# The expert stage of a routed layer: output norms in other places, one of them on another engine, the up-bias as one product

## The reference

```python
eid = argmax(x @ centroids.T)
alpha = sigmoid(sum(x * centroids[eid]))
xn = (x - mu) * rsqrt(var + EPS)
xln = xn * ln_g[eid] + ln_b[eid]
ffn = relu(xln @ w1[eid] + b1[eid]) @ w2[eid] + b2[eid]     # 128 -> 512 -> 128
out = x + alpha * ffn
```

## Time and profile before

| | |
|---|---|
| time, median of 3 runs | 2848.79 us (2848.25 to 2849.33) |
| the profiled execution: time, span | 2853.14 us, 2851.4 us |
| busy: PE, DVE, ACT, POOL | 2018, 1835, 1576, 1163 us |
| mean granted TensorE clock | 0.867 |
| four slots of a pass in the trace: the first scatter | 1159.4 us |
| the last scatter of the stage | 1457.8 us |

### The profile page before, as it was taken

How to read it: one execution, slowest core, us unless ns; L and a number is a source line. 1 busy time by engine, 2 the same in 40 slices (tenths; PEclk the granted TensorE clock), 3 DMA queues, 4 the chain that set the end, 5 groups by cost and what they waited for, 6 DMA issues and landing times. The chain is left out here.

```text
span 2851.4 us, 39979 instructions
## 1 busy us (share of the span) xinstructions
PE 2018.1 (71%) x11854; PEld 1037.9 (36%) x11909; DVE 1834.8 (64%) x3731; ACT 1576.2 (55%) x2903; POOL 1162.6 (41%) x718
## 2 busy tenths in 40 slices
PE   2677777777777763666646787777777777658886
PEld 0344444444444443556522222222222222124432
DVE  5565665555565522222225999999999999946665
ACT  1566666566666642444436666666666666435443
POOL 1111211211221112344325888888888878710000
PEclk7799998889899886888878899989999998878887
DMA  3000000000000001111111111112121111011111
GB/s 121 23 16 20 23 21 27 27 20 20 21 22 20 24 16 33 37 45 41 37 49 47 48 49 41 41 44 56 47 55 40 40 41 49 22 34 30 45 37 45
DMA packets 137060, 105.16 MB, mean 37 GB/s; under 512 B 12872, under 2 KB 130776, under 8 KB 136544
## 3 DMA queue, kind: packets, MB, share of 16 engines
q1 hardware_dynamic: 131424, 89.48, 11.3%
q0 software_dynamic: 5504, 13.90, 1.4%
HBM read 42.18 MB, written 27.59 MB: 24 GB/s over the span
## 5 line engine op out<-in xcount | busy, mean ns | idle before, releaser
L1738 POOL TENSOR_TENSOR hc<-h,c_rep 128x1024 f32<-128x1024 f32 x256 | 602.4, 2369 | 157.4 <-DVE h L1696 150.0
L1696 DVE TENSOR_TENSOR_SCAN h<-decay,bank 128x1024 f32<-128x1024 f32 x256 | 572.6, 2268 | 0.0
L1582 ACT ACTIVATE decay<-bank,neg_a_r 128x510 f32<-128x510 f32 x512 | 322.4, 682 | 323.4 <-PE bank L1473 275.8
L1687 DVE TENSOR_TENSOR bank<-bank,b_rep 128x1024 f32<-128x1024 f32 x256 | 304.3, 1216 | 53.7 <-PE bank L1460 53.0
L1460 PE MATMUL bank<-u,sel_u 128*128 128x512 bf16 x489 | 166.1, 421 | 234.9 <-DVE h L1696 227.9
L613 ACT ACTIVATE es<-bank 128x384 f32<-128x384 f32 x512 | 208.5, 493 | 52.9 <-PE bank L447 52.6
L1460 PEld LDWEIGHTS bank<-u,sel_u 128*128 128x128 bf16 x512 | 33.6, 99 | 408.5 <-DVE h L1696 363.7
L1473 PE MATMUL bank<-d,sel_u 128*128 128x512 bf16 x481 | 168.8, 424 | 6.4 <-ACT decay L1582 2.2
L901 POOL TENSOR_TENSOR xl<-x_in,f_mean_var 128x512 f32<-128x512 f32 x16 | 17.0, 1062 | 363.3 <-ACT f_rstd L604 363.3
L914 POOL TENSOR_TENSOR mag<-mag,one_up 128x512 f32<-128x512 f32 x16 | 20.5, 1282 | 338.7 <-ACT one_up L675 338.7
L1487 PE MATMUL bank<-hc,y_sel 128*32 128x512 f32 x1024 | 146.7, 647 | 4.6 <-POOL hc L1738 4.6
(11 more groups left out here) (333 smaller groups left out, 4727.4 us busy)
## 6 DMA issues: line engine op xcount, KB each, us to landing
xvs<-xv SPq DMA_DIRECT2D x16, 512.0 KB, 3.0
xs<-rows_in_dram SPq DMA_DIRECT2D x72, 68.0 KB
w<-in_w_dram SPq DMA_DIRECT2D x2, 2048.0 KB
x_in<-in_x_dram SPq DMA_DIRECT2D x16, 256.0 KB
xlb_dram<-xl SPq DMA_DIRECT2D x16, 256.0 KB, 2.3
xlb_m<-xlb_dram SPq DMA_DIRECT2D x16, 256.0 KB, 3.8
x_m<-in_x_dram SPq DMA_DIRECT2D x16, 256.0 KB, 3.7
g_xn<-yx_dram SPq DMA_DIRECT2D x16, 256.0 KB
```

The lines of the kernel that those rows point to most:

```text
L1582: act.activation(decay[n % 4][:, i, :, 1:], seq(DL[i])[:, :, 1:], ACT.Exp, scale=c["neg_a_r"][:, hf, g:g + 1]).then_inc(s["n_da"], 1)
L1687: dve.tensor_tensor(pair_of(BD[n % 2]), pair_of(BD[n % 2]), b_rep[p if n < NS else q][:, :].unsqueeze(1).to_broadcast([P, 2, STEP]), ALU.m ...
L1696: dve.tensor_tensor_scan(flat(h[n % 4]), decay[n % 4].rearrange("p i b t -> p (i b t)"), BD[n % 2], 0.0, ALU.mult, ALU.add).then_inc(s["n_ ...
L1738: pool.tensor_tensor(hc[n % 4][:, :, :], h[n % 4][:, :, :], c_rep[p][:, :].unsqueeze(1).to_broadcast([P, 2, STEP]), ALU.mult).then_inc(s[" ...
```

## The change

Five things, none of which alters what is computed:

1. The first norms of a pass are done two in slot 2 and two in slot 3; the sum, the row numbers and `y2` follow in slot 3 and, behind them, the four scatters.
2. The second norm is done by DVE, as (y - mean) x rstd, two in slot 1 and two in slot 2, one pass later than before: a pass has now `norm` (of pass k - 1), `again` (statistics of the sums of pass k - 2, in slot 3, with a semaphore of their own, `mv2`) and `finish` (second norm and scatter of pass k - 3). There is one pass more behind the last.
3. ACT's Ln and Exp stand ahead of slot 1's relu instead of behind its `xls`.
4. The up-bias is one product with 512 columns. `sel` is a one-row-in-32 selector, `b1_split` has the bias with one row for each expert and chunk of 128, and `b2_split` uses every fourth of these rows.
5. In `setup` b_1 is stored to DRAM and loaded back as 32 rows of 128; b_2 is loaded row by row.

```diff
-        b_2 = tmp("b_2", [E, D])
+        b_2 = tmp("b_2", [E * FC, D])
+        b_r = tmp("b_r", [E * FC, P])
         conv_rows = tmp("conv_rows", [P, TAPS, DI])
-        hi = tmp("su_hi", [E, F], bf16)
-        mid = tmp("su_mid", [E, F], bf16)
-        rest = tmp("su_rest", [E, F])
...
-            sp.dma_start(b_2[:, :], dram["b_2"]).then_inc(s["su_expert"], 16)
...
+            sp.wait_ge(s["su_blank"], 1)
+            for e in range(E):
+                sp.dma_start(b_2[FC * e:FC * e + 1, :], dram["b_2"][e:e + 1, :]).then_inc(s["su_b2"], 16)
+            sp.wait_ge(s["su_b1"], 1)
+            sp.dma_start(d["b1"], b_1[:, :]).then_inc(s["su_b1_out"], 16)
+            sp.wait_ge(s["su_b1_out"], 16)
+            sp.dma_start(b_r[:, :], d["b1"].rearrange("e (f p) -> (e f) p", p=P)).then_inc(s["su_b1_in"], 16)
...
+            dve.memset(b_2[:, :], 0.0).then_inc(s["su_blank"], 1)
...
-            chain(dve.tensor_copy(c["sel"][:, :, :], c["sel_cols"][:, 0:E].unsqueeze(2).to_broadcast([P, E, P])))
+            chain(dve.tensor_copy(c["sel"][:, :, :], c["sel_cols"].unsqueeze(2).to_broadcast([P, E * FC, P])))
...
-            chain(dve.tensor_tensor(b_1[:, :], banks[0][0:E, :], b_1[:, :], ALU.add))
-            split3(dve, chain, b_1[:, :], c["b1_split"], hi[:, :], rest[:, :], mid[:, :], E)
-            split3(dve, chain, b_2[:, :], c["b2_split"], hi[:, 0:D], rest[:, 0:D], mid[:, 0:D], E)
+            dve.tensor_tensor(b_1[:, :], banks[0][0:E, :], b_1[:, :], ALU.add).then_inc(s["su_b1"], 1)
 
             for e in range(E):
                 chain(dve.tensor_scalar(c["w_1"][:, e * F:(e + 1) * F], c["w_1"][:, e * F:(e + 1) * F],
                                         e_vec[:, e:e + 1], None, ALU.mult))
-
-
+            dve.wait_ge(s["su_b2"], 16 * E)
+            split3(dve, chain, b_2[:, :], c["b2_split"], hi[:, :], rest[:, :], mid[:, :], E * FC)
+            dve.wait_ge(s["su_b1_in"], 16)
+            split3(dve, chain, b_r[:, :], c["b1_split"], hi[:, :], rest[:, :], mid[:, :], E * FC)
...
-            chain(dve.tensor_copy(c["tile_col"][:, 1, :], of[:, :]))
+            chain(dve.tensor_scalar(c["tile_col"][:, 1, :], of[:, :], float(FC), None, ALU.mult))
...
-            one_pass(eng, 0, 0, 0, True, False, False)
-            one_pass(eng, 1, 0, 1, True, True, False)
-            one_pass(eng, 2, 0, 2, True, True, True)
+            one_pass(eng, 0, 0, 0, True, False, False, False)
+            one_pass(eng, 1, 0, 1, True, True, False, False)
+            one_pass(eng, 2, 0, 2, True, True, True, False)
             with eng.Fori(0, PASSES // 3 - 2) as n:
                 for i in range(3):
-                    one_pass(eng, n * 3 + (3 + i), n + 1, i, True, True, True)
+                    one_pass(eng, n * 3 + (3 + i), n + 1, i, True, True, True, True)
             for i in range(3):
-                one_pass(eng, PASSES - 3 + i, PASSES // 3 - 1, i, True, True, True)
-            one_pass(eng, PASSES, PASSES // 3, 0, False, True, True)
-            one_pass(eng, PASSES + 1, PASSES // 3, 1, False, False, True)
+                one_pass(eng, PASSES - 3 + i, PASSES // 3 - 1, i, True, True, True, True)
+            one_pass(eng, PASSES, PASSES // 3, 0, False, True, True, True)
+            one_pass(eng, PASSES + 1, PASSES // 3, 1, False, False, True, True)
+            one_pass(eng, PASSES + 2, PASSES // 3, 2, False, False, False, True)
...
-                ex = pe.value_load(c["tile_col"][0:1, 1, bass.ds(t, 1)], min_val=0, max_val=E - 1)
-                return col, c["sel"][:, bass.ds(ex, 1), :].rearrange("k a p -> k (a p)")
+                ex = pe.value_load(c["tile_col"][0:1, 1, bass.ds(t, 1)], min_val=0, max_val=(E - 1) * FC)
+                return col, c["sel"][:, bass.ds(ex, FC), :].rearrange("k a p -> k (a p)"), c["sel"][:, bass.ds(ex, 1), :].rearrange("k a p -> k (a p)")
...
-            def up(n, j, first, col, row):
...
                 pe.sem_inc(s["passed"], 1)
-                for f in range(FC):
-                    pe.matmul(bank[:, f * P:(f + 1) * P], c["b1_split"][:, f * P:(f + 1) * P], row, start=f == 0, stop=False, skip_group_check=True)
+                pe.matmul(bank[:, :], c["b1_split"][:, :], rows, start=True, stop=False, skip_group_check=True)
...
-            def one_pass(pool, k, third, r, main, norm, finish):
-                a, b = (r + 2) % 3, (r + 1) % 3
+            def one_pass(pool, k, third, r, main, norm, again, finish):
+                a = (r + 2) % 3
                 for j in range(SLOTS):
                     if main and not is_last(k):
                         copy(k + 1, j, False)
-                    if j == 2 and norm:
+                    if j == 3 and norm:
 
                         pool.wait_ge(s["on"], k)
                         if not (isinstance(k, int) and k < 4):
@@ -1196,11 +1205,11 @@
                         pool.tensor_copy(idx[a][:, :], xs[a][:, :, TOKEN]).then_inc(s["y2"], 1)
                     if j == 3 and finish:
 
-                        pool.wait_ge(s["xno"], k - 1)
+                        pool.wait_ge(s["xno"], k - 2)
                         pool.sem_inc(s["w_passed"], 1)
                         for i in range(SLOTS):
-                            pool.indirect_dma_start(out=d["yx"], out_offset=bass.IndirectOffsetOnAxis(ap=idx[b][:, i:i + 1], axis=0),
-                                                    in_=yx[b][:, i, :], in_offset=None).then_inc(sent[b], 16)
+                            pool.indirect_dma_start(out=d["yx"], out_offset=bass.IndirectOffsetOnAxis(ap=idx[r][:, i:i + 1], axis=0),
+                                                    in_=yx[r][:, i, :], in_offset=None).then_inc(sent[r], 16)
...
-            def one_pass(act, k, third, r, main, norm, finish):
-                a, b = (r + 2) % 3, (r + 1) % 3
+            def one_pass(act, k, third, r, main, norm, again, finish):
...
+                    if j == 1 and (norm or finish):
+
+                        if norm:
+                            act.wait_ge(s["mv"], k)
+                        if finish:
+                            act.wait_ge(s["mv2"], k - 2)
+                        act.activation(ln[:, :], mv[:, :, 1], ACT.Ln, bias=EPS).then_inc(s["ln"], 1)
+                        act.wait_ge(s["ln"], k)
+                        act.activation(rs[:, :], ln[:, :], ACT.Exp, scale=-0.5).then_inc(s["rs"], 1)
+                    if main:
...
-                    if j == 1 and (norm or finish):
-
-                        act.wait_ge(s["mv"], k)
-                        act.activation(ln[:, :], mv[:, :, 1], ACT.Ln, bias=EPS).then_inc(s["ln"], 1)
-                        act.wait_ge(s["ln"], k)
-                        act.activation(rs[:, :], ln[:, :], ACT.Exp, scale=-0.5).then_inc(s["rs"], 1)
-                    if j == 2 and norm:
-                        act.wait_ge(s["nm"], k)
-                        if not (isinstance(k, int) and k == 1):
-                            act.wait_ge(s["y2"], k - 1)
-                        for i in range(SLOTS):
+                    if j >= 2 and norm:
+                        if j == 2:
+                            act.wait_ge(s["nm"], k)
+                            if not (isinstance(k, int) and k == 1):
+                                act.wait_ge(s["y2"], k - 1)
+                        for i in (2 * j - 4, 2 * j - 3):
                             last = act.activation(on[:, i, :], o[a][:, i, :], ACT.Identity, scale=rs[:, i:i + 1], bias=nm[:, i:i + 1])
-                        last.then_inc(s["on"], 1)
-                    if j == 2 and finish:
-                        act.wait_ge(s["nm"], k)
-                        for i in range(SLOTS):
-                            last = act.activation(yx[b][:, i, D:2 * D], yx[b][:, i, 0:D], ACT.Identity,
-                                                  scale=rs[:, SLOTS + i:SLOTS + i + 1], bias=nm[:, SLOTS + i:SLOTS + i + 1])
-                        last.then_inc(s["xno"], 1)
+                        if j == 3:
+                            last.then_inc(s["on"], 1)
...
-            def one_pass(dve, k, third, r, main, norm, finish):
+            def one_pass(dve, k, third, r, main, norm, again, finish):
                 a, b = (r + 2) % 3, (r + 1) % 3
+
+                def second(i):
+                    return dve.tensor_scalar(yx[r][:, i, D:2 * D], yx[r][:, i, 0:D], mv[:, SLOTS + i, 0:1], rs[:, SLOTS + i:SLOTS + i + 1],
+                                             ALU.subtract, ALU.mult)
+
                 for j in range(SLOTS):
                     if main and not (is_last(k) and j + 2 >= SLOTS):
                         features(k, j + 2, is_first(k))
-                    if j == 0:
-                        if norm:
-                            result(k - 1, SLOTS - 1, a).then_inc(s["o_st"], 1)
-                        if finish:
-                            dve.wait_ge(s["y2"], k - 1)
-                            for i in range(SLOTS):
```

(43 more changed lines are left out.)

20 lines of the change are left out of this document (13 added, 7 removed).

## The result

| | before | after |
|---|---|---|
| median of 5 runs, us | 2849.33 (2848.25 to 2857.78) | 2837.27 (2834.74 to 2840.51) |
| ratio | 1 | 0.9953 [0.9936, 0.9970] |
| profiled execution: time, span | 2853.1, 2851.4 | 2840.15, 2838.3 |
| last row scatter of attention ends | 1079.41 | 1085.92 |
| experts' stage, first load of `xs` to first load of `g_xn` | 366.4 | 346.6 |

12.1 us saved, 0.47%, where 31.5 were forecast (2817.3): faster as said and inside the range (2798 to 2842), but less than half of what was forecast. A later set of runs of the same kernel gave 0.9940 [0.9928, 0.9951], 17 us.

The account below looks back on a forecast made before the run. The prediction took a ring between PE and ACT, lengthened by ACT's norms, to bound the experts' stage. 14 x (19.15 - 16.8) = 32.9, + 5.1 - 6.2 - 0.3 = 31.5 us saved: 2817.3 us, range 2798 to 2842.

Parts of the forecast that it names:

- What bounds the kernel: Experts' stage: no engine's busy time but a ring between PE and ACT, lengthened by ACT's output norms; 19.15 us a pass.
- (1): ACT without second norms (1.54 us a pass): tile 2 to tile 3 becomes 3.97 us, the boundary to tile 0 stays 4.73.
- (2): Ln and Exp ahead of tile 1's relu: Exp done at 7.3 us, relu possible at 8.0, wait hidden with 0.7 to spare.
- (4): Scatter burst over tiles 0 and 1: tile 3's down product on time, tile 1's up product late; 16.8 us a pass.
- The prediction's own sign of being wrong: Among the stated signs: Ln waiting for DVE by more than 1 us, which would point to the slower rival.
- (3): Later index copy on POOL: loads for the pass after next arrive at 9.44 us, wanted at 8.88; new wait of 0.56.
- (5): Second norms on DVE, 1.3 to 4.3 us a pass in tiles 1 and 2, where nobody waits: cost 0.
- (6): Up-bias as one product of 512 columns for four of 128: 0, at best 0.2 us at the boundary.
- (7): Ends of the stage: first passes 5.1 us shorter, the work after the last relu 6.2 us longer.
- (8): Setup: wider `sel`, cheaper split of `b_1`, its way through DRAM hidden; +0.3 us, between 0 and +1.5.
- the clock still drops in most passes: Rival for the steady passes: PE's clock still falls, 17.8 us a pass, 2832 us; chance 0.17.
- Still seen late: Slower rival: tile 3's down product still seen late, tile 1's relu 3 us late, PE at 1.2 GHz; 2857 us; chance 0.10.

Follow-up runs that it names:

- a_ln_behind: The changed kernel with Ln and Exp moved back behind tile 1's `xls`, scatters still in a burst of four: 2829.72 us, ratio 0.9931.
- g_second_act: The changed kernel with the second norms back on ACT, two behind tile 2 and two behind tile 3: 2861.46 us, ratio 1.0045.
- b_spread: The changed kernel with a pass's four scatters issued one in each slot instead of in a burst: 2803.25 us, ratio 0.9852.
- i_three: The changed kernel with three scatters in a row behind tile 3's weight copy and the fourth behind tile 1's: 2819.65 us, ratio 0.9902.

## Why the prediction was wrong, point by point

**What bounds the kernel**, a ring of PE and ACT with ACT's norms on it: right. Tile 2 to tile 3 fell from 6.98 to 3.77 us (forecast 3.97).

**(1)** PE's idle time before tile 3's transpose is 1.22 us (forecast 1.3). Tile 2 to 3 was 0.2 dearer in the sum than in the trace: I took the transpose-to-relu time of an early tile, 1.80, where 1.62 was to be had in later ones. The boundary was 0.7 us too cheap: 4.73 at full clock, 5.45 measured, 5.26 with no late signal anywhere. The up product behind PE's 2.3 us of idle time takes 1.35 in the pass above (granted clock 0.64 from 1268 to 1272) and up to 1.91 in others: it is slower than at full clock in 10 of 14 passes, by 0.48 us on average over all. The 0.2 that I added "for passes in which the clock still drops" was the term that should have been 0.5 to 0.7.

**(2) and (4), where the size went.** The step that failed is "Tile 3's down product (5.63) falls near the end of the second scatter, where transposes are seen at once in every pass; I take it as on time". With the longer boundary it ends at 5.8 to 7.6, from the end of the second scatter to the fourth, and it is seen at 9.24, so Exp is done at 10.9 where (2) had 7.3. I had charged a late up product of tile 1 with 0.85 us a pass (16.6 against 15.75), and the clock with 0.2. That up product no longer decides, and with Ln out of its way (a_ln_behind) it is seen only 0.3 to 0.6 us behind its end. The late down product costs 2.0 (17.60 against 15.60). So 15.60 + 2.0 stand for 15.75 + 0.85 + 0.2: 0.8 us a pass, 14 passes, 11 us, the largest part of the miss.

The longer boundary is not what made the product late. Where it does end at the forecast's place it is held as well: in five passes of g_second_act it ends at 5.67 to 5.70 and is seen at 9.14 to 9.28, and in three of the changed kernel's second profile it ends at 5.46 to 5.73 and is seen at 6.96 to 7.72. b_spread and i_three show that the product is safe only if no third scatter follows. The transposes were no measure for it: even those few of the kernel before that end 2.0 to 2.4 us behind the burst's start, the forecast's place, are seen 0.04 to 0.11 us behind their end. Why PE's signals differ so at the same place is open. The prediction's own sign of being wrong was met: Ln waits for DVE by 3.87 us in the pass above.

**(3)** The loads: a wait was forecast in every pass, 0.56 us, where nothing is late. In b_spread, where nothing else is late, ACT's `xns` waits for them now and then (1 to 2 is 3.19 on average, 2.97 without):

```profile
1273.38 0.49 ACT L1245 ACTIVATE xns<-xs 128x128 f32<-128x128 f32 x1 [0.52 <-DMA xs<-rows_in_dram]
```

Right as a mechanism, too dear by 0.35 a pass, because the longer boundary gives the loads time. In the changed kernel two passes wait, 0.9 us each; beside the burst SP's four issues took 5.61 us (1233.44) in one of them and not 3.85.

**(5)** The second norm on DVE at no cost: right. Two took 0.60 us, shorter than the 1.3 to 4.3 for four that attention's rows gave. In b_spread they do lie beside scatters, 30 of them, and these take 0.97 to 0.98 us where all the others take 0.96 to 1.02, so this trace doesn't show the locking that the Trainium skill ("SBUF — State Buffer", "SBUF: two separate sides") describes.

**(6)** The bias product at nothing: right for the time; 0.06 us a tile in the stage.

**(7)** The first passes: -4.9 (forecast -5.1). Behind the last relu: +7.6 (forecast +6.2). The missing 1.4 is a wait of POOL's last sum until earlier scatters have landed, which the kernel before did not have:

```profile
1428.90 1.25 POOL L1204 TENSOR_TENSOR yx<-e_on,xs 128x512 f32<-128x512 f32 x1 [1.61 <-DMA yx_dram<-yx,e_idx]
```

**(8)** Setup: +0.1 (forecast +0.3); `sel` took 2.29 us, b_1's way through DRAM was hidden, as said.

The sum, by the first profiles: 14 x 1.55 + 4.9 - 7.6 = 19 for the 31.5 of the forecast, and 19.8 by the stage (23.7 by the second profile). The medians gave 12 and 17. What lies between has two parts, and neither is the change's. Attention, which it leaves alone, differs by up to 10 us from profile to profile. And every stage is set against the one profile of the kernel before, which took 2853.14 us, 4 to 7 above the medians of that kernel: over all thirteen profiles the saving by the stage is 7 us larger than that by the median on average, and 1.6 larger than that by the profiled times.

**The rivals.** The measured pass (17.60) lies next to that of "the clock still drops in most passes" (17.8, 2832), and the clock did drop at the boundary. But b_spread, where it drops there too (5.26), has a pass of 15.60, so the clock is not what makes it 17.60. "Still seen late" had 0.10 and was in essence what happened, without the loss of clock that made it slower. Its own condition was met: late by more than 0.7 us, 2.1 in the pass above. What it got wrong is that it took the norms on ACT and the late product to meet in one idle time; with the second norms on DVE they don't (g_second_act shows them meeting).

## What to carry to other kernels

A signal that the trace shows late beside a burst is late until about a microsecond behind the end of the burst in most passes, wherever in its second half the work ends: when work is moved relative to a burst, count its new place with the slow clock too, and ask first what a burst cut in pieces would cost, which here was a few lines and worth 25 to 29 us. When a wait for such a signal is moved ahead of other work in a queue, its price is not the lateness less the slack; what stands behind waits either way (here moving it back gave a quarter). An undoing that isn't exact, such as four products with four addresses for four with one, can cost more than what it undoes.

## What the runs showed of the hardware that I had not expected

- Two indirect scatters in a row from GpSimd delay the signal of the down product by 0.5 us at most. With a third or fourth it is held, in most passes until 0.7 to 1.2 us behind the last one's issue, which is within 0.35 us of that scatter's last DMA packet. ACT's signals are held little if at all: in six passes of the profiles of before and after, the `xns` that PE waits for ends inside the hold, and PE goes on 0.13 to 0.37 us later (0.05 elsewhere). Plain DMAs of the same queue, of the same data and for nearly as long, hold nothing.
- The issue of a plain DMA on that queue took 0.54 us, of an indirect one 0.96 to 1.02 (pitch 1.27).
- Four products with a register-based operand address each: their weight loads follow each other at 0.124 us, against 0.044 with one such address for all, 0.3 us a tile and 17 us in the kernel.
- SP's issues beside a burst of scatters stretch from 3.85 to 5.6 us for four; beside spread scatters they took 3.8.
